# Stage changes in a five-stage Mamba and mixture-of-experts kernel: last stores signal semaphores that outlive their stage, constants are waited for where they are used, and the first input products use two PSUM places

## The reference, cut to what matters

```python
def step(state, xs):                       # for each of 1024 positions
    d_t, B_t, C_t, u_t = xs
    dA = jnp.exp(d_t[..., None] * A)
    state = state * dA + (d_t * u_t)[..., None] * B_t[:, None, :]
    y_t = jnp.einsum('ben,bn->be', state, C_t)
    return (state, y_t)
...
y = y + D[None, :, None] * u
y = y * jax.nn.silu(z)                     # z is the layer norm of x
...
x = x + jnp.tanh(g_xattn[0]) * _L0_xattn_ref(ctx_1024, _layernorm(x, axis=-1), ...)
x = x + jnp.tanh(g_ffn[0]) * _L0_ffn_ref(_layernorm(x, axis=-1), ...)
# _L0_ffn_ref: router (top 4 of 32, at most 256 tokens per expert), experts, plus
#   shared = jax.nn.silu(x @ shared_gate) * (x @ shared_up) @ shared_down
```

## Time and profile before

| | us |
|---|---|
| median of 3 runs | 4216.48 |
| lowest and highest | 4215.31, 4220.93 |
| the profiled execution, its own time | 4213.03 |
| its span in the trace | 4211.3 |

### The profile page before, as it was taken

One profiled execution on the slowest core, in us unless ns is written; L12 is line 12 of the kernel. 1 busy time (PEld: TensorE's weight loads), 2 busy tenths in 40 slices (PEclk: granted clock), 3 DMA queues, 4 the chain that ended last, 5 costly groups with the idle time before them and its releaser, 6 DMA issues. The chain is left out here.

```text
span 4211.3 us, 59482 instructions
## 1 busy us (share of the span) xinstructions
PE 3847.6 (91%) x21088; PEld 3151.6 (75%) x21088; DVE 3031.8 (72%) x3701; ACT 2150.4 (51%) x2257; POOL 1799.1 (43%) x1010
## 2 busy tenths in 40 slices
PE   8888378888888888869999989999999999999999
PEld 4444268888778888758888868888888888788887
DVE  7878579999999999867777755555555555455555
ACT  3677678989888889722222234444444444300000
POOL 0355279999999999923333320000000000122221
PEclk9998589999999999979999989999999999999999
DMA  6675753463453553445555557666666666677643
GB/s 231 233 274 224 256 192 108 136 183 116 140 172 116 161 154 113 138 170 175 174 183 184 189 191 245 233 236 232 235 233 234 233 236 238 220 269 262 204 161 121
DMA packets 330294, 821.67 MB, mean 195 GB/s; under 512 B 65872, under 2 KB 111696, under 8 KB 320784
## 3 DMA queue, kind: packets, MB, share of 16 engines
q1 hardware_dynamic: 298240, 752.23, 52.0%
q0 software_dynamic: 31744, 67.23, 5.3%
q10 hardware_dynamic: 144, 0.00, 0.0%
HBM read 603.38 MB, written 245.27 MB: 202 GB/s over the span
## 5 line engine op out<-in xcount | busy, mean ns | idle before, releaser
L1000 POOL TENSOR_TENSOR h<-h,c 128x1024 f32<-128x1024 f32 x512 | 1205.4, 2412 | 33.8 <-DVE h L983 30.8
L983 DVE TENSOR_TENSOR_SCAN h<-da,dbu 128x1024 f32<-128x1024 f32 x512 | 1134.5, 2272 | 67.6 <-ACT dbu L951 51.6
L958 ACT ACTIVATE da<-dl,ad 128x1024 f32<-128x1024 f32 x512 | 588.7, 1150 | 80.7 <-DVE h L983 67.4
L1031 PE MATMUL psy<-ident,h 128*128 128x128 f32 x4096 | 561.4, 281 | 46.1 <-POOL h L1000 26.8
L951 ACT ACTIVATE dbu<-psb 128x1024 f32<-128x1024 f32 x512 | 523.0, 1021 | 61.8 <-PE psb L1021 50.6
L1916 DVE TENSOR_TENSOR wsp<-arena,wsp 128x2048 fp32r<-128x2048 f32 x198 | 447.6, 2288 | 99.9 <-ACT wsp L1869 99.7
L1031 PEld LDWEIGHTS psy<-ident,h 128*128 128x128 f32 x4096 | 446.8, 143 | 79.7 <-POOL h L1000 52.0
L1755 POOL DMA_INDIRECT xg<-scratch_xn,ids x64 | 63.5, 992 | 1034.1 <-PE psT L1773 1010.7
L1869 ACT ACTIVATE wsp<-arena 128x2048 fp32r<-128x2048 f32 x198 | 370.9, 1910 | 24.2 <-DMA arena<-in_w 24.0
L1021 PE MATMUL psb<-m,du_taps 128*128 128x128 f32 x2048 | 288.9, 288 | 62.8 <-ACT dbu L951 62.8
L1021 PE MATMUL psb<-m_first,du_taps 128*128 128x128 f32 x2048 | 292.2, 291 | 47.1 <-ACT dbu L951 22.6
(11 more groups left out here) (208 smaller groups left out, 8100.6 us busy)
## 6 DMA issues: line engine op xcount, KB each, us to landing
arena<-in_w SPq DMA_DIRECT2D x192, 1024.0 KB, 7.1
du_taps<-scratch_duT SPq DMA_DIRECT2D x496, 128.0 KB, 2.9
scratch_duT<-duT SPq DMA_DIRECT2D x64, 512.0 KB, 4.7
c<-scratch_c SPq DMA_DIRECT2D x64, 512.0 KB, 8.6
scratch_xT<-xT_s SPq DMA_DIRECT2D x32, 1024.0 KB, 4.9
scratch_ob<-ob SPq DMA_DIRECT2D x64, 512.0 KB
xT_place<-scratch_xT SPq DMA_DIRECT2D x32, 1024.0 KB, 6.4
xz<-in_x SPq DMA_DIRECT2D x32, 512.0 KB, 5.5
```

The costliest lines, as they stand in the source:

```text
L958: act.activation(da[k % 2][:, :], dl[:, i % 2, :], ACT.Exp, scale=ad[:, i % 2, n:n + 1]).then_inc(s_da, 1)
L983: dve.tensor_tensor_scan(h[:, k % HR, :], da[k % 2][:, :], dbu[:, (k // GN) % 2, k % GN, :], 0.0, ALU.mult, ALU.add).then_inc(s_scan, 1)
L1000: pool.tensor_tensor(h[:, k % HR, :], h[:, k % HR, :], c[:, n, :], ALU.mult).then_inc(s_hc, 1)
L1031: mm = pe.matmul(psy[:, t, :], h[:, k % HR, t * P:(t + 1) * P], ident[:], is_transpose=True, start=(n == 0 and t % 4 == 0), stop=(n == NST ...
```

## The change

Four kinds of edits are made.

**Last stores.** The last store of a stage signals a semaphore in `early` (`du_last`, `gated`, `acc`, `ob`), the end of the stage no longer waits for it, and the first engine of the next stage that touches the memory concerned waits for it there. The store of `a` moves from the end of stage 1 to its third step.

**Constants.** In stage 2 ScalarE takes the tanh of the gate behind unit 8 instead of first. In stages 3 and 5 no engine waits for the constants at its start; TensorE waits before the router's first product, VectorE and ScalarE after the second weight matrix.

**Order in stage 3.** GpSimd adds the first tokens ahead of its memsets, and ScalarE and VectorE take the first weight matrix ahead of the transposed tokens.

**Two PSUM places.** Products 1 and 3 of stage 2 go to `psy`, which holds nothing yet.

```diff
@@ mamba_inputs, SP
-                        .then_inc(s_dust[part], 16)
+                        .then_inc(s_dust[part] if q < Q - 1 else early["du_last"], 16)
@@ step(s)
                 on_tile(s, LOG + 1, store_delta)
+                if s == 2:
+                    sp.wait_ge(s_a2, 1)
+                    sp.dma_start(dr["a"].rearrange("t p n -> p t n"), a_neg[:]).then_inc(s_ast, 16)
...
-            sp.wait_ge(s_a2, 1)
-            sp.dma_start(dr["a"].rearrange("t p n -> p t n"), a_neg[:]).then_inc(s_ast, 16)
...
-                sp.wait_ge(s, 16 * Q)
+                sp.wait_ge(s, 16 * (Q - 1))
@@ selective_scan
+        def product_bank(k):
+
+            if k < GN and k % 2:
+                return psy[:].rearrange("p e (q n) -> p (e q) n", n=GN).rearrange("p (c t) n -> p c t n", t=TB)
+            return psb[:]
...
             def load_u(i):
+                if i == 0:
+                    sp.wait_ge(early["du_last"], 32)
...
-                    .then_inc(s_gst, 16)
+                    .then_inc(s_gst if i < NU - 1 else early["gated"], 16)
...
-            sp.wait_ge(s_gst, 16 * NU)
...
-            act.wait_ge(s_c, 16)
-            act.activation(gate[:], gate[:], ACT.Tanh).then_inc(s_gate, 1)
...
+                if k == GATED_AT:
+                    act.wait_ge(s_c, 16)
+                    act.activation(gate[:], gate[:], ACT.Tanh).then_inc(s_gate, 1)
...
-            dve.wait_ge(s_gate, 1)
+            dve.wait_ge(early["du_last"], 32)
...
-                after(pe, s_ev, k)
+                after(pe, s_ev, k - 1 if k <= GN else k)
@@ shared_pass
+            if route:
+                sp.wait_ge(early["gated"], 16)
...
+                    .then_inc(early["acc"] if route and isinstance(t, int) and t == TT - 1 else s_acst[par], 16)
...
                 add_x(0, 0)
+                pool.memset(ones[:], 1.0)
+                pool.memset(run[:], 0.0)
...
+                pool.wait_ge(early["ob"], 16)
...
-            pe.wait_ge(s_c, 16 * NCONST)
-            if route:
-                pe.wait_ge(s_init, 1)
...
             if route:
+                weight_head(0)
                 x_head(0, 0, 0)
+                weight_head(1)
+                gate_tanh()
+                weight_head(2)
...
+                norm(0, 0, 0)
+                weight_rest(0)
+                x_rest(0, 0)
+                weight_rest(1)
+                dve.wait_ge(s_c, 16 * NCONST)
...
+                weight_rest(2)
@@ experts
+                    .then_inc(early["ob"] if t and isinstance(e, int) and e == NE - 1 else s_obst[t], 16)
...
+            act.wait_ge(early["acc"], 16)
```

More of the change, by code:

```diff
@@ L971, in gate_tile @@
             def gate_tile(i):
+                if i == 0:
+                    dve.wait_ge(s_gate, 1)
                 dve.wait_ge(s_szl, i * 16 + 16)
@@ L1075, in shared_pass @@
             xT = sb("xT", [P, 2, 2, KH, P], F32R)
+        ac = sb("ac", [P, 2, H])
+        if not route:
+            x1t = sb("x1t", [P, 2, H])
         sg = sb("sg", [P, HB])
         hT = sb("hT", [P, 2, KF, P], F32R)
-        ac = sb("ac", [P, 2, H])
         psG, psU = ps("psG", [P, HB]), ps("psU", [P, HB])
@@ L1242, in _ @@
             for s in (*((*s_xnst, *s_x1st, *s_xtst) if route else ()), *s_acst):
-                sp.wait_ge(s, 16 * TT // 2)
+                sp.wait_ge(s, 16 * TT // 2 - (16 if route and s is s_acst[1] else 0))
         if route:
@@ L1247, in _ @@
             def _(pool):
[L1248 to L1251, removed]
                 def add_x(j, par):
@@ L1261, in _ @@
                 add_x(0, 0)
+                pool.memset(ones[:], 1.0)
+                pool.memset(run[:], 0.0)
+                pool.memset(step[:], 2 * P)
+                pool.memset(zero[:], 0).then_inc(s_init, 1)
                 add_x(0, 1)
@@ L1362, in pair @@
                     if route:
+                        if first:
+                            pe.wait_ge(s_c, 16 * NCONST)
+                            pe.wait_ge(s_init, 1)
                         after(pe, s_posr, t)
@@ L1402, in _, with gate_tanh, weight_head @@
         def _(act):
-            act.wait_ge(s_c, 16 * NCONST)
-            act.activation(gate[:], gate[:], ACT.Tanh).then_inc(s_tanh, 1)
+            def gate_tanh():
+                act.wait_ge(s_c, 16 * NCONST)
+                act.activation(gate[:], gate[:], ACT.Tanh).then_inc(s_tanh, 1)
+                act.wait_ge(s_tanh, 1)
+            def weight_head(m):
+                for half in range(2):
+                    act.wait_ge(early["w3"][m][half] if m < 2 else s_raw[half], 16)
+                    act.activation(wsp[:, m, 0, halves[half]], raw[:, m % 2, halves[half]], ACT.Copy).then_inc(s_whi, 1)
             def x_head(t, par, j):
@@ L1450, in _ @@
             if route:
+                weight_head(0)
                 x_head(0, 0, 0)
[L1452 to L1457, removed]
+                weight_head(1)
+                gate_tanh()
+                weight_head(2)
+            else:
+                act.wait_ge(early["ob"], 16)
+                gate_tanh()
             turns(act, TT // 2, pair, last=True, first=2)
@@ L1499, in finish @@
                 dve.tensor_tensor(ac[:, par, :], ac[:, par, :], x1t[:, par, :], ALU.add).then_inc(s_sum, 1)
-            dve.wait_ge(s_c, 16 * NCONST)
-            dve.wait_ge(s_tanh, 1)
+            if not route:
+                dve.wait_ge(s_tanh, 1)
             if route:
@@ L1738, in _ @@
             store_rows(NE - 1, 1)
-            for s in s_obst:
-                sp.wait_ge(s, 16 * NE)
+            sp.wait_ge(s_obst[0], 16 * NE)
+            sp.wait_ge(s_obst[1], 16 * (NE - 1))
         @block.gpsimd
@@ L1979, in program @@
                      w3=[[sem(f"early_shared{i}_half{half}") for half in range(2)] for i in range(2)],
-                     w4=[[sem(f"early_expert{i}_half{half}") for half in range(2)] for i in range(2)], xT=sem("early_transposed"))
+                     w4=[[sem(f"early_expert{i}_half{half}") for half in range(2)] for i in range(2)], xT=sem("early_transposed"),
+                     du_last=sem("last_du_stored"), gated=sem("last_gated_stored"), acc=sem("last_acc_stored"),
+                     ob=sem("last_rows_stored"))
         mamba_inputs(nc, io, dr, ident, arena, m0, taps, early)
```

24 lines of the change are left out of this document (11 added, 13 removed).

## The result

| | before | changed |
|---|---|---|
| median us, 6 runs each | 4215.90 | 4188.57 |
| lowest and highest | 4211.77, 4221.62 | 4185.47, 4198.43 |
| the profiled execution, its own time | 4213.03 | 4191.98 |

The ratio of the times is 0.9935, with a 95% interval of 0.9924 to 0.9947: 27.3 us less, where 28.2 were forecast. All eleven runs of the changed kernel have a median of 4191.95, some 24 to 26 us under the medians of before (4215.9 to 4218.4 in four series). The total was forecast well; one of its six terms had the wrong sign.

The account below looks back on a forecast made before the run. TensorE in stage 3 and GpSimd in stage 2 were taken to set the pace, so time saved before that counts; 4.9 + 2.9 + 13.5 + 2.1 + 2.3 + 2.5 = 28.2 off 4216.5 gave 4188 us, range 4180 to 4198.

Parts of the forecast that it names:

- Stage 1 to 2, the end (4.9): Release of stage 2 no longer waits for `a` and the last du pair to land; 4.9 us saved.
- the rival by which the ends do not move: Stage ends: SP's drain may include transfers under way, so landings stay in the path; total 4200 us, chance 0.12.
- Stage 2, the start (2.9): Ramp of stage 2: first scan 6.6 us earlier, but TensorE then waits for `u`, so only 2.9 us kept.
- lower bound of 0 on this term: Stage 2's start: the least gain allowed, 0 us, if `u` lands still later; the upper bound was 9.5.
- The rival that the first scans' gain is kept: Stage 2's start gives 7 to 9.5 us instead of 2.9; total 4183 us, chance 0.13.
- Stage 2 to 3 (13.5): From the last gated store to stage 3's second norm: earlier release, late constants and new order save 13.5 us.
- 1.2 for contention in norm: Stage 3's first norm: 1.2 us added because GpSimd's second add runs beside it; bounds 0 and 2.9.
- the 8.1 us of the gated store: End of stage 2: SP's wait for the last gated store to land, so the release comes 8.1 us earlier.
- Stage 3's and stage 4's ends (2.1, 2.3): Ends of stages 3 and 4: SP's waits for the last stores, after all engines are done, save 2.1 and 2.3 us.
- Stage 5's start (2.5): TensorE starts stage 5 at the release instead of when the gate has landed; 2.5 us saved.
- The clock bonus: Stage 5's start: up to 2 us more if TensorE started at its upper clock level; taken as 0.
- The slower rival: Stage 3: SP's wait for the last gated store delays the third matrix's load and everything behind; kernel slower, chance 0.02.

Follow-up runs that it names:

- after_again: The changed kernel unaltered, run a second time in another series: median 4192.06 us beside 4216.81 for the kernel before, ratio 0.9945.
- u_early: Against the changed kernel, SP's first load of `u` moved behind the eighth row of `c` instead of all sixteen: median 4182.42 us, ratio 0.9910 to before.
- u_early_again: Changed kernel with the first load of `u` behind the eighth row of `c`, run a second time: median 4185.23 us, ratio 0.9924 to before.
- ends_only: Against the changed kernel, constants, stage 3's order and one PSUM place as before; only last stores and early `a` kept: 4203.85 us, ratio 0.9969 to before.

## Why the prediction was right, and where it was not

The number held, and the mechanisms of five of the six terms.

**Stage 1 to 2, the end (4.9).** The mechanism was right: SP's drain did not wait for the transfer (0.12 us at the end of stage 2, with 6.8 us of the gated store still to come), and the rival by which the ends do not move falls. The term is 4.1: the release came 2.27 behind the last issue and not 1.36.

**Stage 2, the start (2.9).** This step failed, with its sign: -2.0, and -2.5 in after_again. Its first half was right, TensorE stood at the skip term for the 7 to 9 forecast. Two things were then wrong. `u` was taken to land 36.9 after the release as before ("None of this moves against the release"), and landed at 38.9, so that TensorE went on at 39.0 (2.1); this is one of the prediction's own signs of being wrong. And the products behind the wait were costed as before, while TensorE had fallen to its lower level in the standstill: from the first skip matmul to scan 12 it took 9.77 instead of 7.18 (2.6). Together that is 4.7 of the 4.9 from +2.9 to -2.0. The lower bound of 0 on this term was therefore wrong as well: a wait of 8.7 us on TensorE should have carried the price of the clock, as the last stage's rows showed it. The Trainium skill has it, in "TensorE: Matmul & The Clock Gate", section "HAM oscillation": a wait for a DMA lets the clock fall, so that the work behind it starts slow; this case's trace agrees, 1.95 us for a product instead of 1.12. The rival that the first scans' gain is kept falls in this kernel, and is true of the ramp of u_early (49.2 - 42.0 = 7.2).

**Stage 2 to 3 (13.5).** 15.0 and 13.4 in two profiles. The first add waited for the tokens' landing, as forecast; 1.2 for contention in norm was not paid. For the 8.1 us of the gated store the prediction also quotes a formula, which gives 3.2. The Trainium skill has it in "DMA: Bandwidth & Descriptors", section "Anatomy of one DMA", for transfers that GpSimd issues. This store was issued by SP; it took 7.2 us from issue to landing in the changed kernel and 6.5 to 8.5 in the nine kernels that do not wait for it. One sub-term hides in the sum: the ends alone give 4.2 here and not 8.1, and the rest comes from constants and order, of which the order is 4 to 5.

**Stage 3's and stage 4's ends (2.1, 2.3).** 4.95 - 2.91 = 2.0, and 4.46 - 2.19 = 2.3.

**Stage 5's start (2.5).** 2.58 - 0.04 = 2.5. The clock bonus was rightly left out of the sum: the clock fell 1.2 us after the start instead of being low at it, and the fourteenth product came 4.6 after the first instead of 4.8.

**The sum.** 4.1 - 2.0 + 15.0 + 2.0 + 2.3 + 2.5 = 23.9 by the first profile, and 4.1 - 2.5 + 13.4 + 2.0 + 2.3 + 2.5 = 21.8 by after_again. The spans of the profiles before and after (4211.3 and 4190.2) lie 21.1 apart: stage 1 took 4.9 longer and the rest of stage 2 2.3 longer, and the middles of stages 3 to 5 together 4.3 less. All runs together say 24 to 26. The first series' 27.3 lies above that, so that the closeness of 28.2 to it is partly luck: a term 4.9 too high met a series of runs some 3 us low. The slower rival, SP held by the gated store, did not show: the third matrix was asked for at 1803.43, when the first matrix's first rest was done, and the gated store had landed at 1797.5.

**The rest of stage 2.** From the thirteenth multiplication to the last gated tile the profiles took between 1195 and 1202 us (1207 with the wait for the du taps in u_early_again), with no edit in that part. The profiles say where this arises. GpSimd is busy for 1176.9 to 1177.6 us of it in all twelve, and stands for 18.1 (ends_only) to 29.7 (u_early_again). Its longest stands in the part are where the second, third and fourth of the four sequences begin, in all twelve (u_early_again has the one at the du taps besides). The second sequence in the timeline of the changed kernel:

```profile
854.87 1.93 PE L1034 MATMUL psb<-m_first,du_taps 128*128 128x128 f32 x8 [4.12 <-DMA du_taps<-scratch_duT]
...
861.27 2.39 POOL L1013 TENSOR_TENSOR h<-h,c 128x1024 f32<-128x1024 f32 x1 [2.86 <-DVE h L996]
```

It is the ramp's pattern again: TensorE waits for a load, its next product takes 1.93, and GpSimd stands. In ends_only TensorE waits 1.92 there and GpSimd stands 0.82. Why a load is late in one execution and not in the other stays open, and no experiment moved it. The part took 1195.4 to 1201.3 us in the five kernels with one PSUM place and 1199.1 to 1207.0 in the seven with two. So the prediction's premise, that a microsecond saved before the pace is reached is saved for good, is not shown for stage 2.

## What to carry to other kernels

When a start is made faster, list the loads behind it by landing time, because the first engine that now comes too early stands; TensorE here paid twice, in the wait and in the clock behind it. Ask also which loads the faster start triggers earlier, and what they may collide with. Before a second buffer is added to a ramp, ask whether the ramp's loads are in the order in which they are needed. Moving one load ahead of eight rows was worth more than the two places, and only with it did they gain in the ramp; in the whole time their gain was not seen. And where single executions differ by 4 to 5 us in a part that no edit touches, terms of 2 us are read from the timeline against a mark close by, and the total from many runs.

## What the runs showed of the hardware

Stage 1 does the same work in all executions, and takes 505.5 to 506.7 us or 509.0 to 511.4. Part of the difference lies in TensorE's granted clock behind a stretch in which it waits. Busy times by stretches, first of the kernel before, then of the changed one:

```profile
116.00:120.00 4.00, 2.15 (x12) 1.21 (x11) 3.93 (x4) 2.95 (x4) 0.00 (x0) 1.00 0.96 322
120.00:122.00 2.00, 2.00 (x8) 1.13 (x9) 1.75 (x5) 1.43 (x2) 0.00 (x0) 1.00 1.03 422
122.00:124.00 2.00, 2.00 (x6) 0.95 (x5) 1.68 (x8) 0.11 (x1) 0.00 (x0) 1.00 0.81 330
```

```profile
116.00:120.00 4.00, 2.93 (x13) 1.51 (x12) 3.89 (x4) 3.28 (x5) 0.00 (x0) 1.00 0.95 326
120.00:122.00 2.00, 1.22 (x6) 1.05 (x6) 1.86 (x4) 0.81 (x2) 0.00 (x0) 0.77 1.00 397
122.00:124.00 2.00, 2.00 (x3) 0.66 (x2) 1.72 (x5) 1.33 (x2) 0.00 (x0) 0.50 1.00 408
```

TensorE stands 1.85 us between 116 and 122 in both (4.00 - 2.15, and 1.07 + 0.78), and only in the second does its clock fall to 0.50 behind it; its sixteen matrix multiplications there take 8.50 us instead of 7.03. The one difference found in the timelines is that this work begins 0.96 us later (a product at 116.07 instead of 115.11). The Trainium skill, "TensorE: Matmul & The Clock Gate", section "What's actually happening", says that the chip's looks at activity run freely and do not start with the kernel. The twelve profiles agree with it in that no edit tells the long ones from the short, but no run here shows the looks themselves.

The clock records of the twelve traces, summed over the same stretch, part the two groups: TensorE has its lower level for 132.2 to 136.2 us in the six short stages and for 139.2 to 146.8 in the six long ones, 8.1 more on average. At half speed that is an estimate of 4.0 us of TensorE's work, and the long stages are 4.3 longer on average. This fits, but no experiment moved the clock alone.
